# Long attention with probabilities as weights, layer norms by tiles, and a new order of loads in a perceiver kernel

## The reference

```python
x = x + _L0_xattn_ref(_layernorm(x), ctx_768, ...)   # ternary weights, int8 activations, two rounds over the context
x = x + _L0_attn_ref(_layernorm(x), ...)             # rotary, 16 heads of 8, causal, 32 tokens
x = x + _L0_ffn_ref(_layernorm(x), ...)              # gate, 8 added weight sets, gelu
x = x + _L1_xattn_ref(_layernorm(x), ctx_768, ...)   # the long attention
x = x + _L1_attn_ref(_layernorm(x), ...)
x = x + _L1_ffn_ref(_layernorm(x), ...)              # a fixed linear map by FFT
```

```python
attn = jnp.clip(jnp.einsum('bhqd,bhkd->bhqk', q, k) * scale, -CLAMP, CLAMP)
attn = jax.nn.softmax(attn, axis=-1)
attn = jnp.where(jnp.any(jnp.isnan(attn)), 1.0 / Nkv, attn)
x = jnp.einsum('bhqk,bhkd->bqhd', attn, v).reshape(B, Nq, Cq)
return x @ Wo + bo
```

## Time and profile before

| | |
|---|---|
| median of 3 runs | 376.3 us (375.72 to 378.17) |
| profiled execution | 377.07 us, of this the span 375.3 us |
| mean granted clock of TensorE | 0.899 |
| PE busy | 293.2 us (78%), 3040 instructions |
| PE weight loads | 179.4 us (48%), 3041 |
| DVE busy | 263.1 us (70%), 653 |
| ACT busy | 175.4 us (47%), 316 |
| POOL busy | 49.0 us (13%), 80 |

### The profile page before, as it was taken

One profiled execution on the slowest core, in us unless ns is written; L12 is line 12 of the kernel. 1 busy time (PEld: TensorE's weight loads), 2 busy tenths in 40 slices (PEclk: granted clock), 3 DMA queues, 4 the chain that ended last, 5 costly groups with the idle time before them and its releaser, 6 DMA issues.

```text
span 375.3 us, 7739 instructions
## 1 busy us (share of the span) xinstructions
PE 293.2 (78%) x3040; PEld 179.4 (48%) x3041; DVE 263.1 (70%) x653; ACT 175.4 (47%) x316; POOL 49.0 (13%) x80
## 2 busy tenths in 40 slices
PE   0038484979897996659999996797999999957853
PEld 0013312526453965624445553274666666644742
DVE  3799898957789856658742445696588888675733
ACT  2869495953637644220100000457677777712420
POOL 2041332500000153430002001110000000002001
PEclk9999697989999999659999999687899999995975
DMA  7980000000000699792000000000000000000000
GB/s 178 247 332 1 0 2 0 0 2 3 0 3 1 161 211 218 167 372 79 1 0 1 0 2 0 0 1 2 4 4 3 4 5 3 4 2 0 2 3 29
DMA packets 5357, 19.22 MB, mean 51 GB/s; under 512 B 961, under 2 KB 2113, under 8 KB 4673
## 3 DMA queue, kind: packets, MB, share of 16 engines
q1 hardware_dynamic: 5314, 18.63, 18.1%
HBM read 12.07 MB, written 0.26 MB: 33 GB/s over the span
## 4 chain that ended last, share of the span: by engine, by line
PE 56%; DVE 26%; issue 7%; ACT 4%; DMA 4%; SPq 1%; POOL 1%; POOLq 0%; DVEq 0%; ACTq 0%
PE PS L1057 53%; DVE sm L670 5%; DMA cx<-ctx_in 4%; DVE yq L677 3%; DVE big L730 3%; DVE xn L577 2%; PE PS L1246 1%; DVE yq L739 1%; SPq L253 1%; POOL rstd L297 1%; ACT xT L476 1%; DVE w L833 1%; DVE sm L832 1%; DVE sm L789 1%; ACT sa L368 1%
## 5 line engine op out<-in xcount | busy, mean ns | idle before, releaser
L992 DVE TENSOR_REDUCE sm<-PS 128x1 f32<-128x512 f32 x64 | 43.3, 685 | 11.7 <-PE PS L1057 9.5
L532 ACT ACTIVATE yq<-PS,sm 128x512 f32<-128x512 f32 x44 | 30.1, 687 | 13.9 <-PE PS L1057 13.7
L297 POOL TENSOR_TENSOR rstd<-veps,mhalf 128x4 f32<-128x4 f32 x6 | 6.1, 1018 | 210.1 <-DVE veps L574 210.1
L1057 PE MATMUL PS<-diag,ones 128*128 128x128 f32 x14 | 4.6, 424 | 36.1 <-DVE diag L603 25.6
L1057 PE MATMUL PS<-sa,w 128*32 128x36 f32 (+1 forms) x320 | 30.8, 280 | 2.4 <-ACT w L499 2.4
L368 ACT ACTIVATE big<-PS,cols,sm 128x512 f32<-128x512 f32 (+1 forms) x40 | 32.0, 875 | 0.7 <-PE PS L1057 0.7
L1057 PE MATMUL PS<-yq 128*128 128x384 f32 x96 | 31.1, 486 | 0.0
L476 ACT COPY xT<-PS 128x512 f32<-128x512 f32 x5 | 2.9, 586 | 58.2 <-PE PS L1246 58.1
L1057 PE MATMUL PS<-yq,big 99*128 99x128 f16 x256 | 26.2, 225 | 2.8 <-ACT yq L536 1.5
L1057 PE MATMUL PS<-big,yq 96*128 96x512 f16 x64 | 25.6, 406 | 1.9 <-ACT yq L368 1.9
L1057 PEld LDWEIGHTS PS<-yq,big 99*128 99x128 f16 x256 | 19.4, 100 | 11.9 <-issue 6.7
(11 more groups left out here) (244 smaller groups left out, 627.1 us busy)
## 6 DMA issues: line engine op xcount, KB each, us to landing
big<-yq SPq DMA_DIRECT2D x12, 512.0 KB, 10.4
cx<-ctx_in SPq DMA_DIRECT2D x8, 384.0 KB, 10.8
w<-w_in SPq DMA_DIRECT2D x9, 256.0 KB, 9.5
yq<-w_in SPq DMA_DIRECT2D x1, 2304.0 KB, 8.8
wa<-wa_in SPq DMA_DIRECT2D x1, 1156.0 KB, 18.5
sa<-wx_in SPq DMA_DIRECT2D x1, 768.0 KB, 14.6
rows<-rows_in SPq DMA_DIRECT2D x1, 580.0 KB, 16.2
tern<-rows_in SPq DMA_DIRECT2D x1, 512.0 KB, 4.4
```

The lines of the kernel that those rows point to most:

```text
L297: pool.tensor_tensor(rstd[:, :], veps[:, :], mhalf[:, :], ALU.pow).then_inc(s["ln_rstd"], 1)
L532: nc.scalar.activation(pt(i), PS[:, ST_BANK[i % 2], :], ACT.Exp, scale=s1(M_ES))\
L992: V.tensor_reduce(s1(M_MX + i % 8), PS[:, S_BANK[i % 3], :], AX, ALU.max, negate=True)\
L1057: return nc.tensor.matmul(o, lhsT, rhs, start=start, stop=stop, **kw)
```

## The change

- **Outputs.** The 32 queries of one head become the weights (128x32 of the probabilities), and a block of 9 columns moves: the 8 values of its head and a one. There are 16 matmuls for a quarter of a batch's keys in place of 8. Values are stored in blocks of 9 columns (`values_of`); they take more room, so they start 448 columns ahead of the context, and the first chunk lies over masks and cosines in `cst`. ACT copies values with a stride, POOL writes the ones (`denominator_ones`). Four batches share a bank. For each four batches DVE takes 16 reciprocals a row and multiplies once; PE transposes the result with 16 matmuls of 32x32; DVE copies it to `qTs`. `sum_heads` and `sum_denominators` go.
- **Maxima.** `split_maximum` goes to POOL, as five steps that wait for each other; DVE waits before it overwrites a maximum.
- **Layer norm.** Statistics, aggregation, epsilon, root and normalisation go tile by tile; POOL takes four roots of 128x1.
- **Factor rows.** A 64-column tile is set once by POOL, and a transfer with repeated source writes the rows, last on SP before the outputs.
- **SP's queue.** The key copies go in two halves of 12 transfers, the first when half of the keys are there and the first cross attention is done, ahead of `tb2`. `w1` no longer waits for the key copies; `w2` comes behind it.
- **Room.** `gbc`, `mb1`, `gtok` and `lin` move into other tiles.

```diff
--- before.py
+++ after.py
...
+C_V0 = C_MK0
+C_LIN = 840
+C_FACTOR = 968
+HV = HD + 1
+VC = 4 * H * HV
+V_LEAD = 448
...
-        cx = sb("cx", [128, CP])
+        cv = sb("cv", [128, V_LEAD + CP])
...
+        cx = cv[:, V_LEAD:V_LEAD + CP]
+        lin = cst[:, C_LIN:C_LIN + 128]
...
+        factors = cst[:, C_FACTOR:C_FACTOR + 64]
...
+        def values_of(c, n=1):
+            return cst[:, C_V0:C_V0 + VC] if c == 0 else cv[:, VC * (c - 1):VC * (c - 1 + n)]
...
+            def copy_keys(half):
+                c0 = CP // 2 * half
+                sp.wait_ge(s["kp_h"], NCH // 2 * (half + 1))
+                sp.wait_ge(s["kp_l"], NCH // 2 * (half + 1))
+                for r in range(R):
+                    for part in range(3):
+                        sp.dma_start(kst[32 * part:32 * part + 32, r, c0:c0 + CP // 2],
+                                     khl[32 * r:32 * r + 32, part % 2, c0:c0 + CP // 2]).then_inc(s["kst_done"], 16)
+            sp.wait_ge(s["pv_ps"], 2 * T)
+            copy_keys(0)
             sp.wait_ge(s["f2_ps"], 1)
             sp.dma_start(tb2, rows_in[:, R_END:R_END + E * D]).then_inc(s["ld_tb2"], 16)
...
+            copy_keys(1)
             sp.wait_ge(s["sa_pv"], 1)
             for e in range(1, E1):
                 sp.dma_start(w1[:, e * FF:(e + 1) * FF], w1_in[:, e * FF:(e + 1) * FF]).then_inc(ld_ws[e - 1], 16)
+            sp.wait_ge(s["kst_done"], 6 * R * 16)
+            sp.dma_start(w2, w2_in.rearrange("p (c e d) -> p c e d", c=FC, e=E1)).then_inc(s["ld_w2"], 16)
+            sp.wait_ge(s["consts"], 2)
+            sp.dma_start(big[96:99, :, :].rearrange("p a (k n) -> p (a k) n", n=64),
+                         factors[96:99, :].unsqueeze(1).broadcast_to([3, 16 * NCH, 64])).then_inc(s["key_ones"], 16)
...
-                pool.wait_ge(s["ln_veps"], n + 1)
-                pool.tensor_tensor(rstd[:, :], veps[:, :], mhalf[:, :], ALU.pow).then_inc(s["ln_rstd"], 1)
+                for t in range(T):
+                    pool.wait_ge(s["ln_veps"], T * n + t + 1)
+                    pool.tensor_tensor(rstd[:, t:t + 1], veps[:, t:t + 1], mhalf[:, t:t + 1], ALU.pow)\
+                        .then_inc(s["ln_rstd"], 1)
...
+            pool.memset(factors[:, :], MAX_FACTOR_PAIR).then_inc(s["consts"], 1)
...
-            pool.wait_ge(s["pv_ps"], 2 * T)
-            pool.wait_ge(s["k_evp"], 1)
-            link(pool.memset(big[96:99, 0, :], MAX_FACTOR_PAIR))
+            def denominator_ones(part):
+                c0, n = VALUES[part][0][0], len(VALUES[part])
+                pool.wait_ge(s["vp_ev"], c0 + n)
+                if c0 == 0:
+                    pool.memset(values_of(0).rearrange("p (j n) -> p j n", n=HV)[:, :, HD:HV], 1.0).then_inc(s["v_ones"], 1)
+                    c0, n = 1, n - 1
+                pool.memset(values_of(c0, n).rearrange("p (j n) -> p j n", n=HV)[:, :, HD:HV], 1.0).then_inc(s["v_ones"], 1)
+            def split_maximum(b):
+                k = b % 2
+                mx, scaled, rest = s1(M_MX + R * k, R), mscaled[:, k, :], mrest[:, k, :]
+                high, mid, low = (mparts[:, k, :, m] for m in range(3))
+                pool.wait_ge(s["ls_max"], R * b + R)
+                if b >= 2:
+                    pool.wait_ge(s["ls_rows_ps"], b - 1)
+                link(pool.tensor_scalar(scaled, mx, 1.0 / MAX_FACTOR, None, ALU.mult))
+                link(pool.tensor_copy(high, scaled))
+                link(pool.tensor_tensor(rest, scaled, high, ALU.subtract))
+                link(pool.tensor_copy(mid, rest))
+                pool.tensor_tensor(low, rest, mid, ALU.subtract).then_inc(s["ls_parts"], 1)
+            denominator_ones(0)
             rstd_of(2)
-            pool.wait_ge(s["ln_rstd"], 3)
-            pool.memset(big[96:99, 1, :], MAX_FACTOR_PAIR).then_inc(s["key_ones"], 1)
-            pool.wait_ge(s["key_ones"], 1)
...
+            for b in range(2):
+                split_maximum(b)
+            denominator_ones(2)
+            for b in range(2, B):
+                split_maximum(b)
...
-                    nc.scalar.copy(cx[:, chunk(c)], PS[:, bank, :]).then_inc(s["vp_ev"], 1)
+                    nc.scalar.copy(values_of(c).rearrange("p (j n) -> p j n", n=HV)[:, :, 0:HD],
+                                   PS[:, bank, :].rearrange("p (j d) -> p j d", d=HD)).then_inc(s["vp_ev"], 1)
...
             def layer_norm(n, out_tile, done=None, product=None, stats=True):
+                def tile_stats(t):
                     if product is not None:
+                        dve.wait_ge(s["x_tile"], n_tiles[0] + t + 1)
+                    V.bn_stats(bn[:, t, :], x[:, t, :]).then_inc(s["ln_stats"], 1)
+                def tile_moments(t):
+                    if stats:
+                        dve.wait_ge(s["ln_stats"], n_stats[0] + t + 1)
+                    V.bn_aggr(mv[:, t, :], bn[:, t, :]).then_inc(s["ln_mv"], 1)
+                def tile_variance(t):
+                    dve.wait_ge(s["ln_mv"], T * n + t + 1)
+                    V.tensor_scalar(veps[:, t:t + 1], mv[:, t, 1:2], LN_EPS, None, ALU.add).then_inc(s["ln_veps"], 1)
+                lag = 0 if product is None else 1
+                for i in range(T + lag + 2):
+                    if product is not None and i < T:
                         ps_sem, k = product
...
+                        dve.wait_ge(ps_sem, T * k + i + 1)
+                        V.tensor_tensor(x[:, i, :], x[:, i, :], PS[:, i, 0:128], ALU.add).then_inc(s["x_tile"], 1)
+                    if stats and 0 <= i - lag < T:
+                        tile_stats(i - lag)
+                    if 0 <= i - lag - 1 < T:
+                        tile_moments(i - lag - 1)
+                    if 0 <= i - lag - 2 < T:
+                        tile_variance(i - lag - 2)
+                if product is not None:
+                    n_tiles[0] += T
+                n_stats[0] += T if stats else 0
                 for t in range(T):
...
+                    dve.wait_ge(s["ln_rstd"], T * n + t + 1)
...
-            def split_maximum(b, n):
...
-            def sum_heads(g, n):
...
+            def lo_sums(t):
+                return PS[:, O_BANK[t % 2], 0:4 * R * HV].rearrange("p (g n) -> p g n", n=HV)
+            def reciprocals(t):
+                dve.wait_ge(s["lo_ps"], 4 * t + 4)
+                V.reciprocal(s1(M_NAN + 16 * t, 16), lo_sums(t)[:, :, HD]).then_inc(s["lo_rd"], 1)
+            def normalise(t):
+                dve.wait_ge(s["lo_rd"], t + 1)
+                V.tensor_tensor(tmp[:, t, :].rearrange("p (g d) -> p g d", d=HD), lo_sums(t)[:, :, 0:HD],
+                                s1(M_NAN + 16 * t, 16).unsqueeze(2).broadcast_to([128, 16, HD]), ALU.mult)\
+                    .then_inc(s["lo_norm"], 1)
+            def to_features(t):
+                dve.wait_ge(s["lo_tp"], t + 1)
+                V.tensor_copy(qTs[:, tile(t)], PS[:, O_BANK[t % 2], 256:384]).then_inc(s["lo_ev"], 1)
+            for b in range(B + 1):
...
+                        if r == 0 and b >= 2:
+                            dve.wait_ge(s["ls_parts"], b - 1)
...
+                    if b % 4 == 3 and b >= 7 and r in (1, 2):
+                        (reciprocals, normalise)[r - 1](b // 4 - 1)
+                    if b % 4 == 0 and b >= 8 and r == 2:
+                        to_features(b // 4 - 2)
...
+            reciprocals(T - 1)
+            normalise(T - 1)
+            dve.wait_ge(s["lo_norm"], T)
+            V.tensor_tensor(s1(M_NAN, 64), s1(M_NAN, 64), s1(M_NAN, 64), ALU.not_equal).then_inc(s["nan_max"], 1)
+            dve.wait_ge(s["nan_max"], 1)
             V.tensor_reduce(s1(M_V), s1(M_NAN, 128), AX, ALU.max).then_inc(s["nan_max"], 1)
-            sum_heads(g, 2)
-            dve.wait_ge(s["nan_max"], 1)
+            dve.wait_ge(s["nan_max"], 2)
             V.tensor_scalar(diag[:, :], ident, s1(M_V), None, ALU.mult).then_inc(s["gm_diag"], 1)
-            sum_heads(g, 3)
-            sum_heads(g, 4)
+            to_features(T - 1)
             dve.wait_ge(s["gm_ps"], n_gmax[0] + 1)
             V.tensor_reduce(s1(M_V + 1), PS[:, 7, 0:128], AX, ALU.max).then_inc(s["nan_max"], 1)
-            sum_heads(g, 5)
-            dve.wait_ge(s["nan_max"], 2)
+            dve.wait_ge(s["nan_max"], 3)
             link(V.tensor_scalar(flags[:, 1:2], s1(M_V + 1), 0.0, None, ALU.is_gt))
-            dve.wait_ge(s["sum_step"], 6 * B // 2)
+            dve.wait_ge(s["lo_ev"], T)
...
             def outputs(b, k):
-                if b % 2 == 0 and b >= 4 and k == 0:
-                    pe.wait_ge(s["sum_step"], 6 * (b // 2 - 2) + 4)
-                    pe.wait_ge(s["den_sum"], b // 2 - 1)
+                if b % 4 == 0 and b >= 8 and k == 0:
+                    pe.wait_ge(s["lo_ev"], b // 4 - 1)
                 if b == 0 and k == 0:
                     pe.wait_ge(s["vp_ev"], NCH)
+                    pe.wait_ge(s["v_ones"], 4)
                 if k == 0:
                     pe.wait_ge(s["lt_exp"], R * b + R)
...
```

(46 more changed lines are left out.)

99 lines of the change are left out of this document (8 added, 91 removed).

## The result

The changed kernel takes 389.2 us (385.8 to 393.0, four runs) against 376.2 for the kernel before in the same group: 1.0305 times as long, 95% interval 1.0208 to 1.0402. (Every ratio in this text leaves out executions more than 1.5% above the fastest of the same kernel, here the one of 393.0.) Forecast were 360.7 us, range 352 to 371. The profiled execution took 385.81 us (span 384.0; before 375.3).

What follows compares the result with a forecast made beforehand. TensorE was taken as the bound, in the first layer's feed-forward and the long attention. Terms: -6.0 - 1.9 - 10.2 - 0.3 + 2.8 = -15.6 us, so 360.7 us, range 352 to 371.

Steps and rivals of the forecast that it cites:

- Part 1: Third layer norm and first gate: DMA for memsets ends a stall, -6.0 us; gate at 2.4 GHz, -1.9 us.
- Part 2: Long attention outputs with probabilities as weights: unit 0.95 us, 0.17 less than before; -10.2 us in all.
- I take 9.1: 32 x 9.1 = 0.29: Long attention outputs: 32 pairs of weight load and matmul at 9.1 ns each, 0.29 us a unit.
- The 80 pairs: Self-attention's product with values: pairs starting between 147.2 and 147.9 us, taken as the pace for the new outputs.
- 160 records in 0.73 us, 4.6 ns each: 0.48 + 0.34 = 0.82, hidden: Long attention: TensorE's instruction queue needs 0.82 us a unit for 74 records, below the unit's 0.92.
- Rival (b): Long attention: issue is the bound, 19.5 ns a pair, unit 1.25 us, total +5.0, 381.3 us; chance 0.07.
- its 390 us: Long attention: at the skill page's 25 ns a pair, unit 1.44 us, run near 390 us; chance 0.03 more.
- rival (c): Long attention: fewer streamed columns, clock granted 0.50, +33 us throughout the loop, near 402 us; chance 0.05.
- Part 3: Long attention: maxima split on GpSimd in 1.5 us, hidden; head sums leave VectorE; -0.3 us at the attention's end.
- Part 4: Layer norms by tiles: normalising products contend with one-column roots, +0.7 us each, +2.8 us for four.

Runs made afterwards that it cites:

- part 1 alone: Kernel before with factor rows by DMA, key copies in halves and the new SP queue order, nothing else: 367.9 us, 0.978.
- experiment 2: Changed kernel plus four f32 products of 128 columns (eight pairs) a unit into unread PSUM: 400.5 us, 1.062 of the kernel before.
- Experiment 3: Changed kernel with f16 probabilities and values, 16 output pairs a unit instead of 32: 374.6 us, 0.997 of the kernel before.
- Experiment 7: Changed kernel with the old outputs plus 48 waits a unit for a semaphore reached long ago: 532.3 us, 1.423 of the kernel before.
- experiment 8: Changed kernel and the changed kernel with each score product done twice, timed in one group: 392.7 us, 1.045, and 385.3 us, 1.025.
- experiment 4: Changed kernel with each 512-column score product of the long attention done twice: 383.4 us, 1.031 of the kernel before.
- 6: Changed kernel with the old outputs plus 24 one-column bf16 products a unit into unread PSUM: 392.5 us, 1.059 of the kernel before.
- experiment 5: Changed kernel with f16 probabilities and values, and each score product done twice: 362.3 us, 0.978 of the kernel before.

## Why the prediction was wrong, by its own steps

**Part 1: right.** -6.0 and -1.9 stood against -7.5 measured alone (375.4 to 367.9 by the medians). The copy was forecast 6.0 sooner and came 9.25 sooner in the changed kernel, of which 2.4 were there at the `qT` copy; counted from that it is 6.9, and 6.5 in part 1 alone. The gate ran at a granted 1.00, and gate to gated input took 159.42 - 155.62 = 3.8 us, as forecast.

**Part 2: wrong, and it is the step that failed.** "I take 9.1: 32 x 9.1 = 0.29" is true of one burst: the changed kernel's outputs start at 263.77 and the next scores at 264.14, 0.37 us with the edge:

```profile
263.11 0.39 PE L1084 MATMUL PS<-big,yq 96*128 96x512 f16 x1
263.45 0.39 PE L1084 MATMUL PS<-yq,big 99*128 99x128 f16 x4
263.77 0.44 PE L1084 MATMUL PS<-cv,w 128*32 128x9 f32 x32
264.14 0.39 PE L1084 MATMUL PS<-big,yq 96*128 96x512 f16 x1
```

It is not true of a stream of them. The 80 pairs behind 9.1 ns came after 1.2 us in which TensorE waited for its weights, and nothing but their own 0.7 us was asked of whatever hands out the instructions. That is also where "160 records in 0.73 us, 4.6 ns each: 0.48 + 0.34 = 0.82, hidden" broke: a burst's pace was used as the pace of 64 units. The sustained one is 35 ns a pair, so 38 pairs take 1.3 us against 1.18 for the 22 before. Rival (b) had this mechanism, issue as the bound, with a chance of 0.07, and its +0.13 us a unit (1.12 to 1.25) is what came (1.18 to 1.30). That the size fits is luck: its 19.5 ns were the pace of 32x32 products and only for the outputs, and the pace here is 35 ns over every pair. Its counter-argument, "9.1 ns held over 80 pairs", was the same burst. The Trainium skill (TensorE: Matmul & The Clock Gate, "Wait — 56ns, not 53.3ns?") has about 25 ns from start to start as a floor; the bursts here go below it (8.4 ns a pair in experiment 2), and the streams at 35 ns stay above it, so neither follows it. That its 390 us lay nearest is luck too, since more than half of the loss is the clock's by the estimate below. Three smaller slips change nothing: the unit of 1.12 left out the maxima's rows, eight times 0.15 are 1.2 and not 1.0, and rival (c) adds up to 404 and not 402.

**Rival (c), the clock: right in kind, dismissed for a bad reason.** "TensorE has no gap in the loop" was taken as evidence against 0.50. Experiment 3 has no gap and 0.50, experiment 2 has gaps of over 1 us and 1.00. What both of these kernels at 0.50 share, the changed one and that of experiment 3, is that the streamed output columns were gone; adding columns to each of them brought 1.00 back, in the changed one not in every execution. Experiment 7 shows the other way down, long idle with the columns there. How much of either it takes isn't shown. The two causes don't add up: at 1.2 GHz a unit takes 1.62 us, more than the 1.3 that the instructions need, so the idle vanishes from 278 us on and the clock takes its place as the bound. How large each is: in the group where both stood, the new outputs cost 392.8 - 367.2 = 25.6 us (a further run of the changed kernel, quoted below). In that run's trace the clock is 0.50 from 251 us on, through nearly all of the 51 full units. At full clock they would have taken 1.30 us for 1.62, 16 us less (an estimate; the 9.0 us of experiment 8 are its lower bound, since that kernel pays for the added columns). The other 9 or 10 us are the pace, and without the clock's fall the changed kernel would be at 377 to 380 us, still a little slower than the 374 to 375 before, in spite of part 1. That is near rival (b)'s 381.3.

> The changed kernel once more, beside the other kernels of this group on the same chip: about 1.03 times the kernel before, as at first (1.0305). It is here so that its clock and idle can be compared within one group; if the clock's fall is part of the cost and not the whole of it, its TensorE has 30 matmul records a us or fewer at full clock and 24 a us at half clock again.

It took 392.8 us, 1.050 (1.044 to 1.057).

**Part 3: right.** Five steps on GpSimd take 1.3 us, from 264.52 to 265.84 (forecast 1.5), and nobody waits for them:

```profile
264.52 0.22 POOL L379 TENSOR_SCALAR mscaled<-sm 128x4 f32<-128x4 f32 x1 [4.79 <-DVE sm L1032]
...
265.63 0.21 POOL L383 TENSOR_TENSOR mparts<-mrest,mparts 128x4 f16<-128x4 f32 x1
```

The idle of 0.84 us before the maxima's rows at 262.79 looks like such a wait and isn't one: it is booked to issue, and the same idle falls into the middle of an output row elsewhere. From the last output's end (343.63) to the first predicated copy (346.56) are 2.9 us, forecast 2.7, at half clock.

**Part 4: the price was wrong, harmlessly.** Products beside a running root take 0.35 us, not the feared 0.6, and TensorE transposes each tile as it comes. From the first root to the end of the last product are 2.49 us (151.69 to 154.18) against 2.17 in the earlier trace rows, less the earlier start: nothing, where +0.7 each was forecast. What the memset did to VectorE in the earlier trace rows one-column roots don't do; their contention can't be read off from it.

What stays open: what sets the 35 ns. The traces hint at the delivery of instructions. In the middle of a row of like matmuls TensorE goes from a burst to a full stop, and it does so at half clock too. The chain of the changed kernel, at its last outputs:

```profile
339.67 1.90 PE PS L1084 x128
341.57 1.56 issue
343.13 0.52 PE PS L1084 x21
```

128 pairs pass in 1.90 us, 14.8 ns each, at 1.2 GHz, and then nothing for 1.56 us. A limit of the pair in the array would space them evenly; this is argued, not shown. The queue of instruction packets tells less than it seems to. In 260 to 320 us (packets, MB, share), in the kernel before and in that of experiment 4:

```profile
q8 instruction: 12, 0.20, 1.4%
```

```profile
q8 instruction: 16, 0.26, 1.8%
```

Experiments 2 and 6 have 15 and 16, experiment 3 has 11; in experiment 2 the idle returns once in about 4 us, the time of one packet. But experiment 5, nearly without idle, has 15 too, and so has the changed kernel, mostly at half clock. The packets follow the number of records, 93 to 114 matmuls each, and don't single out the kernels that wait. Experiment 7 was to tell delivery from a limit in the array and failed.

## What to carry to other kernels

Price a stream of small matmuls by the sustained pace of the records, not by a burst that follows an idle: count weight loads and matmuls per unit of the loop, and where a change trades few wide matmuls for many narrow ones, keep it under about 28 pairs a us as measured here. A change that removes streamed columns from the engine that is the bound can also take its clock: ask what granted clock the leaner loop will have, and compare full-clock and half-clock unit times, each against the old unit. Split a bundle: here the transfer in place of the memsets, with the new order of the queue, was worth 7.5 us alone, and the version with all but the new outputs (364.4 us, 0.967, later 0.983) beats both kernels. Before a gain of a few us in a stage is credited to a change, count it from a mark ahead of the change: two traces differed by 2.4 us there.

## What was not expected of the hardware

- More work made a kernel faster: 64 extra score products took the f16 kernel from 0.997 to 0.978 of the kernel before, and the changed one from 392.7 to 383.7 us in the executions that kept their clock, by the granted clock.
- One kernel, the doubled scores, kept its clock in seven executions and lost it in four, 19 us apart.
- The granted clock stood at 0.50 from 276 to 357 us, although TensorE was shown as busy without a break for 50 of them (277.65 to 328.12).
- A wait for a semaphore that was long reached costs TensorE 54 ns, six times a pair in a burst.
